# A feed-forward block's first bias moved from VectorE into the product, with three steps of its turn reordered

## The reference, cut to what matters

```python
def act_quant_fake(x):
    scale = 127.0 / jnp.clip(jnp.max(jnp.abs(x), axis=-1, keepdims=True), 1e-05)
    return jnp.clip(jnp.round(x * scale), -128.0, 127.0) / scale
def weight_quant_fake(w):
    scale = 1.0 / jnp.clip(jnp.mean(jnp.abs(w)), 1e-05)
    return jnp.clip(jnp.round(w * scale), -1.0, 1.0) / scale
def bitlinear(x, w, b):
    dqx = act_quant_fake(x)
    dqw = weight_quant_fake(w)
    return jnp.einsum('btd,hd->bth', dqx, dqw) + b
...
h = layernorm(x, ln1_g, ln1_b)
h = bitlinear(h, w1, b1)                    # 256 -> 1024
h = jax.nn.gelu(h, approximate=False)
h = layernorm(h, ln2_g, ln2_b)
h = bitlinear(h, w2, b2)                    # 1024 -> 256
...
pre = gate_in @ ifgate_w.T + ifgate_b       # gates of the next layer, from its layernormed input
```

## Time and profile before

| | before |
|---|---|
| median of 3 runs | 385.18 us (384.57 to 385.5) |
| profiled execution | 385.09 us, span 383.3 us |
| TensorE busy | 326.1 us, 85% |
| VectorE busy | 297.4 us, 78% |
| ScalarE busy | 283.5 us, 74% |
| GpSimd busy | 235.2 us, 61% |
| mean granted TensorE clock | 0.99 of full speed |

### The profile page before, as it was taken

The page is one execution under the profiler, slowest core; times in us unless marked ns, Lnnn a source line. Parts: engine busy times, 40 slices in busy tenths (PEclk is TensorE's granted clock), DMA queues, the critical chain, the costliest instruction groups (busy, mean ns, idle before and its releaser), DMA issues.

```text
span 383.3 us, 9007 instructions
## 1 busy us (share of the span) xinstructions
PE 326.1 (85%) x2933; PEld 225.1 (59%) x2933; DVE 297.4 (78%) x1014; ACT 283.5 (74%) x594; POOL 235.2 (61%) x278
## 2 busy tenths in 40 slices
PE   7899789999999999756767778678877999999976
PEld 6777566766767665424445545446445666666654
DVE  3899755786988986898998998986446787787884
ACT  5666486677667787837798989887668888888753
POOL 1213543877888897578998898982005546546560
PEclk9999999999999999989899999999999999999999
DMA  7999999999956600000000000000001212212101
GB/s 228 287 286 270 258 226 206 251 215 255 206 109 150 120 1 5 1 0 0 0 2 3 1 0 2 1 2 0 2 15 29 43 43 44 56 43 43 43 16 55
DMA packets 44141, 33.67 MB, mean 88 GB/s; under 512 B 19904, under 2 KB 40256, under 8 KB 43968
## 3 DMA queue, kind: packets, MB, share of 16 engines
q1 hardware_dynamic: 44096, 33.11, 36.1%
HBM read 24.71 MB, written 8.39 MB: 86 GB/s over the span
## 4 chain that ended last, share of the span: by engine, by line
PE 41%; DVE 26%; issue 17%; ACT 8%; DMA 4%; POOL 2%; SPq 1%; DVEq 0%; POOLq 0%; ACTq 0%
PE PS L1751 4%; DVE sm L812 4%; PE PS L1743 4%; PE PS L1409 4%; DMA QT<-scr_k 3%; PE PS L1515 3%; DVE sm L784 3%; PE PS L1481 3%; PE PS L1490 3%; PE PS L1572 3%; PE PS L1713 2%; PE PS L1498 2%; PE PS L1736 2%; DVE negm L673 2%; PE PS L1702 2%
## 5 line engine op out<-in xcount | busy, mean ns | idle before, releaser
L673 DVE TENSOR_REDUCE negm<-PS 128x4 bf16<-128x512 f32 x64 | 41.0, 685 | 13.1 <-PE PS L1490 12.9
L1166 ACT ACTIVATE pT<-PS 128x512 f32<-128x512 f32 x64 | 36.4, 595 | 16.7 <-PE PS L1481 15.9
L499 POOL TENSOR_TENSOR kst<-kst,rows 128x1024 f32<-128x1024 f32 x16 | 38.0, 2372 | 7.9 <-ACT kst L1229 7.9
L1306 ACT ACTIVATE lnT<-PS,Atok 128x128 f32<-128x128 f32 x128 | 36.5, 370 | 2.0 <-DVE lnb L930 0.8
L1621 PE MATMUL PS<-identf,w2f 128*128 128x128 f32 x128 | 17.9, 284 | 18.2 <-ACT w2f L1252 18.2
L516 POOL TENSOR_TENSOR kst<-kst,rows 128x1024 f32<-128x1024 f32 x14 | 33.1, 2367 | 0.0
L538 POOL TENSOR_TENSOR smd<-smd,mhalf 128x1 f32<-128x1 f32 x16 | 9.0, 564 | 37.0 <-DVE smd L998 37.0
L1515 PE MATMUL PS<-pT,vx 128*32 128x128 f32 x512 | 27.3, 285 | 1.8 <-ACT pT L1166 1.8
L544 POOL TENSOR_TENSOR rr<-ms,mhalf 128x8 f32<-128x8 f32 x16 | 26.3, 1646 | 1.9 <-DVE ms L1012 1.9
L1621 PEld LDWEIGHTS PS<-identf,w2f 128*128 128x128 f32 x128 | 14.1, 143 | 22.6 <-ACT w2f L1252 22.4
L930 DVE SCALAR_TENSOR_TENSOR lnb<-PS,lnT 128x512 f32<-128x512 f32 x32 | 20.6, 683 | 8.1 <-PE PS L1713 5.9
(11 more groups left out here) (237 smaller groups left out, 1014.8 us busy)
## 6 DMA issues: line engine op xcount, KB each, us to landing
scr_q<-qpart SPq DMA_DIRECT2D x8, 384.0 KB, 3.5
scr_k<-kpart SPq DMA_DIRECT2D x8, 384.0 KB, 4.6
X<-in_x SPq DMA_DIRECT2D x8, 256.0 KB, 4.9
CTXT<-in_ctxT SPq DMA_DIRECT2D x8, 256.0 KB, 4.7
vx<-in_ctx SPq DMA_DIRECT2D x16, 128.0 KB, 2.7
out<-rest SPq DMA_DIRECT2D x16, 128.0 KB, 1.7
rows<-in_rows SPq DMA_DIRECT2D x1, 1544.0 KB, 14.2
qst<-scr_q SPq DMA_DIRECT2D x8, 192.0 KB, 5.3
```

What stands on the lines that cost most here:

```text
L499: gp.tensor_tensor(n2[q.slot], n2[q.slot], ln2g, ALU.mult).then_inc(b_g2, 1)
L673: v.tensor_reduce(negm[f.slot % 2][:, 4 * hg:4 * hg + 4], PS[:, 2 + hg % 2, :].rearrange("p (h k) -> p h k", h=4), AX_X, ALU.max, negate=T ...
L1166: s.activation(pT[:, hg, :], PS[:, hg % 2, :], ACT.Exp, scale=float(DH0) ** -0.5).then_inc(a_e, 1)
L1306: last = s.activation(dT[half][:, cols], PS[:, half, cols], ACT.Exp, scale=1.0, bias=Atok[:, n.b, h:h + 1])
```

## The change

The addition of b1 leaves VectorE. Instead b1 is split into three bf16 parts and laid out in rows (b1p, repeated in every quarter of 32 partitions), and 1/(u m) of each token is split in the same way (ivp, 32 columns a block, six of them used). One product with the identity turns ivp of four blocks at once into PSUM, ScalarE copies it out (ivT), and `up` gets two more products with 32 rows each that add b1/(u m) to its sum. Gelu then reads PSUM itself, with uw = u m as its scale. hidden is gone.

```diff
@@ TensorE
-                done(pe, b_hb, a, 0)
+                if a.b % 4 == 0:
+                    pe.wait_ge(b_ip, 2 if a.b < 12 else 4)
+                    t.matmul(PS[:, 4, 256:384], ivp[:, a.b:a.b + 4, :].rearrange("p a k -> p (a k)"), identb[:],
+                             start=True, stop=True).then_inc(b_it, 1)
+                done(pe, b_gl, a, 0)
...
+                pe.wait_ge(b_iT, a.b // 4 + 1)
+                for n in range(2):
+                    last = t.matmul(PS[:, 2 + n, :], ivT[a.b // 4 % 2][quarter, :], b1p[quarter, n * 512:(n + 1) * 512],
+                                    start=False, stop=True)
@@ VectorE
-            def hidden(b):
...
-                if b and b.b > 1:
-                    hidden(b)
...
+            def bias_rest(i):
+                dve.wait_ge(b_bm, i + 1)
+                v.scalar_tensor_tensor(out=b1r, in0=b1p[:], scalar=b1m[:, 2 * i:2 * i + 1], in1=b1r,
+                                       op0=ALU.mult, op1=ALU.add).then_inc(b_b1, 1)
...
+            def inverse_parts(low, high):
+                some = slice(low, high)
+                dve.wait_ge(c_z, 1)
+                dve.wait_ge(l_c, l_links(high))
+                ilink(v.tensor_scalar(uw[:, some], unit1[:, some], wmean[:, 0:1], None, ALU.mult))
+                ilink(v.reciprocal(iv[:, some], uw[:, some]))
+                for k in range(3):
+                    ilink(v.tensor_copy(ivp[:, some, k], iv[:, some]))
+                    if k < 2:
+                        ilink(v.tensor_tensor(iv[:, some], iv[:, some], ivp[:, some, k], ALU.subtract))
@@ ScalarE
+                if a.b % 4 == 0:
+                    act.wait_ge(b_it, a.b // 4 + 1)
+                    s.activation(ivT[a.b // 4 % 2][:], PS[:, 4, 256:384], ACT.Copy).then_inc(b_iT, 1)
...
             def gelu(b):
-                act.wait_ge(b_hb, b.b + 1)
+                act.wait_ge(b_m1, b.b + 1)
```

More of the change, by code:

```diff
@@ L201, in build @@
         hT = sb("hT", [128, KC, S], BF16)
+        b1p = sb("b1p", [128, F], BF16); b1m = sb("b1m", [128, 3]); ehot = sb("ehot", [128, 32])
+        uw = sb("uw", [128, NB]); iv = sb("iv", [128, NB]); ivp = sb("ivp", [128, NB, 32], BF16)
+        ivT = [sb(f"ivT{i}", [128, S], BF16) for i in range(2)]
         sm1 = [sb(f"sm1_{i}", [128, 16]) for i in range(4)]
@@ L1239, in turn_b @@
                     columns(a)
+                if b:
+                    gelu(b)
                 if g:
@@ L1256, in turn_b @@
                                  ACT.Copy).then_inc(b_QT, 1)
-                if p and p.b == 0:
-                    normed(p, tau)
-                if b:
-                    gelu(b)
-                if p and p.b > 0:
+                if p:
                     normed(p, tau)
```

127 lines of the change are left out of this document (78 added, 49 removed).

## The result

The changed kernel takes 412.02 and 414.03 us, against 384.57 to 385.5 for the kernel before: a ratio of 1.072, with a 95% interval of 1.068 to 1.076. Two more of its runs took 419.6 and 420.5, with a mean TensorE clock of 0.94 instead of 0.97, and are left out of the ratio. The forecast had the sign right and the size wrong: 402.2, with a range that ended at 408.

The account below looks back on a forecast made before the run. It took a ring on VectorE through hidden to bound the feed-forward turn, with PRET's wait for the gates' product next. Seam 3.05, turns 10.0, tail 3.3 and attention 0.7 gave +17.0 on 385.09: 402.2 us, range 394 to 408.

Parts of the forecast that it names:

- A steady turn: Middle of the feed-forward stage: PRET waits 1.0 us for the gates' product, so a turn takes 6.40 us, 0.34 more.
- 7.63 against 7.91: Turns 8 and 12: ScalarE's ivT stands ahead of gelu and waits for its product, so each takes 7.91 us.
- the sum: Turns 8 to 19, from h2T of turn 8 to that of turn 20: 78.58 us against 68.59, +10.0 us.
- rival A: At the seam, TensorE's clock falls to 1.2 GHz after its pause: +2.7 us, 404.9 us in all; chance 0.18.
- Turns 17 and 18: Late feed-forward turns: 6.40 us for turn 17, and 5.78 for turn 18, set by u2 and its turning.
- The tail: After the last h2T: gates, QT and n3 follow one another, tanh at 11.25 us instead of 7.97, +3.3 us.
- The seam and the early turns: Attention's end to h2T of turn 8: late ivp delays `up` and gelu, partly recovered, +3.05 us.
- the ring of 5.05: Early turns behind the seam: `up`, eight keep_busy, columns, hT and gelu make a ring of 5.05 us.
- the ring on VectorE: Old kernel's feed-forward turn of 6.06 us: set by VectorE's hidden, gelu and its statistics; removing hidden's 1.28 us opens it.
- rival C: Feed-forward turns: gates' product ready before gelu ends, turn falls to GpSimd's 5.61 us, 377 to 380 in all; chance 0.03.
- inverse_parts of turn 9 has about 1.8 us of room: Turn 9 on VectorE: the small instructions have about 1.8 us of room; an unknown term of up to 2 us.
- The attention turns: Ahead of the seam: bias_rest takes 1.2 to 1.3 us where a ternary step took 0.7; +0.7 us (0 to 1.9).

Follow-up runs that it names:

- e14: Changed kernel's bias form in the old order, with filled seam, inverse_parts(12, 16) spread over turns 9 to 11, and ScalarE's QT behind gelu; 387.8 us, ratio 1.007.
- e8: Kernel before with hidden left on VectorE, only TensorE's and ScalarE's turn in the changed kernel's order; 404.3 us, ratio 1.048.
- e4: Changed kernel plus products that nobody reads in TensorE's pauses at the seam, `up` of block 2 and turns 16 to 19; 412.1 us, ratio 1.069.
- e10: As e9, but ScalarE copies hT (and ivT) behind u2 instead of ahead of PRET; 397.2 us, ratio 1.032.
- e11: As e10, with unread products filling the seam and inverse_parts(0, 12) ahead of VectorE's ternary step; 393.1 us, ratio 1.019.
- e5: Changed kernel's bias in PSUM, but the old order of TensorE and ScalarE, and ivp's turning product ahead of columns; 404.4 us, ratio 1.048.
- e12: As e5, without the two 32-row products that add the bias (output lacks b1); 396.8 us, ratio 1.029.
- e16: Kernel before with one move, ScalarE's QT behind gelu; 384.4 us, ratio 0.998.
- e1: Changed kernel with the gates' product back at block t-7 at the end of TensorE's turn; 403.6 us, ratio 1.045.
- e9: As e7, with inverse_parts(12, 16) cut in four, in turns 7 to 10 ahead of gelu's statistics; 397.0 us, ratio 1.030.
- e7: As e5, with inverse_parts(0, 12) one attention turn earlier and `up` of block 1 and columns of block 2 in their old places; 400.2 us, ratio 1.036.
- e17: As e14, with the nine instructions of inverse_parts(12, 16) right behind scale2 in turns 8 to 11; 384.6 us, ratio 0.999.

## Why the prediction was wrong

**The direction and the mechanism held.** PRET's wait for the gates' product, its line (L1679), ivT's wait for L1515, ivp as what `up` waits for at the seam, and GpSimd and VectorE under the turn were as written. A steady turn of 6.31 against 6.40, 7.63 against 7.91 and gelu from PSUM at 0.99 start to start (e14, a steady turn) against 1.04 are small misses. Over the twelve turns from 8 to 19 the sum was 3.0 short: 2.7 for the clock, 0.8 for a table load and 0.7 for turn 10, less 1.2 that these misses give back. e8 shows 6.31 with hidden in place, too: the new order alone sets it.

**The step that failed first is the clock.** The sum put it at nothing, and rival A priced it at one place and 2.7 us, with a chance of 0.18. The rows show falls at five places from the seam on. The miss is 9.9 us at the stage's end (26.94 against 17.05), and it sits in four terms, the last of which, the attention, stands further below:
- Turns 17 and 18, put at 6.40 and 5.78, took 7.77 and 7.85. e4, which kept the clock there, had 6.31 and 6.58: 2.7 us are the clock. The remaining 0.8 of turn 18 is a table load of 1.28 ahead of h2T that the sum had overlooked.
- The tail, put at 11.25, took 12.19, with the clock at 0.67 from 296 to 300. In e8 it took 14.4.
- The seam and the early turns, put at +3.05, cost 8.0 (S8 +9.77, of which 1.78 were there at hT(0)). That is the largest miss, 5 us. ivp came 2.6 later than forecast: 1.1 is the attention's and stands outside the 5, 0.7 is that nine linked instructions took 2.3 and not 1.6, and the rest that they began later. From ivT to gelu it took 6.55, not 5.2, since L1523, L1526 and L1624 ran at half the clock and ScalarE's yT waited 1.30 for L1571 behind them. From there on the deficit grew instead of shrinking: +3.9 at the first gelu, +4.3 at `up` of block 2, +6.2 at that of block 3. Between the two `up` took 2.5 where the ring of 5.05 had 1.31, and keep_busy, with columns behind it, 2.45 where it had 1.89, both in the fall at 172 to 176.

How much of the seam is the clock and how much is order isn't settled for the changed kernel itself. For the old order two pairs of runs give a size, though neither pair changes the clock alone: removing the wait for yb and filling the pauses together gave 5.4 us from hT(0) to S5 (e10 to e11), and leaving the 32-row products away gave 4.6 (e5 to e12).

**The reading of the kernel before was wrong in one step**, though the forecast's number stood on it only in part: "What sets the turn is the ring on VectorE", with hidden in it, and "taking 1.28 us off VectorE therefore opens the ring". Since gelu starts 0.16 after hidden's end, the two looked linked; but QT's step on ScalarE ends there too. In the old order the relief was worth 0.03 us a turn (e5 against before), and 0.11 once QT had left the ring (e14 against e16). In the new order it is another matter: e1, with PRET's wait gone and gelu ahead of u2, took 5.65 in the turns that kept the clock, which is the turn of rival C (377 to 380). How much of these 0.41 us is hidden's absence and how much gelu's place no run tells apart, since none has e1's order with hidden in it. C's condition, the gates' product ready before gelu ends, isn't met in the changed kernel. The early turns' recovery, where GpSimd at 5.6 was taken as the bound, didn't come: the deficit was 3.9 at the first gelu and 6.7 at S8.

**The turns' extra, turn 10.** "inverse_parts of turn 9 has about 1.8 us of room" was wrong: the subtraction of four columns took 2.19 and the turn 7.11. The text had named the mechanism (and the Trainium skill's sentence on it) and left it out of the sum. The Trainium skill, SBUF — State Buffer, section "SBUF: two separate sides", says that VectorE and GpSimd share a pair of ports which goes to one of them for a whole instruction, and that a VectorE instruction with one SBUF input asks for it too when it runs in a fast two-port mode. By it a cast can be the victim as well; e9's cast, 2.17 beside GpSimd's sum of 2.36, agrees.

**The attention turns**, put at +0.7 (0 to 1.9), gave +1.78. Of that 1.2 to 1.3 came at 44 to 53, where the clock fell to 0.50 in the profiled runs of the changed kernel, e1, e5, e7, e9 and e11 and in none of the others. The change hardly touches that stretch, so which event tips it stays open. The rest, 0.5, is what several things leave: bias_rest took 2.11 and 2.10 at its two places (128.06 and 141.73, forecast 1.2 to 1.3), beside GpSimd's copies of 2.02, which made two turns 0.5 and 0.7 longer, and an earlier turn was 0.5 shorter than in the trace of before, as it is in e8's.

Not shown by any run: what the changed kernel would take with the clock held up throughout. Taking off 2.7 and 0.9 us at the end and up to 5 at the seam would leave it near 403, close to the forecast, but e4, with fillers at some places, had falls at others (227 to 231 and 241 to 244), so this is argued only.

## What to carry to other kernels

Before crediting a change with time off a busy engine, write down the ring that closes a turn step by step, start to start, and see that it sums to the turn; an instruction that ends just ahead of a step of the ring needn't be in it. In a kernel that is bound by latency a wait of under 1 us put in every turn can cost twice: itself, and TensorE's clock behind the longer pauses (e8 had both). The falls move with every edit, so compare whole kernels, and before calling a turn's length steady, look at the granted clock in it and at a turn that kept the full clock (e1: 6.88 and 5.65). Small linked VectorE instructions belong where GpSimd runs nothing long, however short they are (e17 against e14: turns 10 and 11 of 5.86 and 5.85, not 7.37 and 7.44).
